# Empty slots left out of the product-row fetches, and fetch runs throttled to four, in a graph network kernel

## The chip, the cores and the metric

One NeuronCore of a Trainium2 chip runs the whole kernel. The metric is device time in microseconds for one execution, lower is better.

## The reference

The input is a graph of 1250 nodes (rows of 768 floats) and 20000 edges, each with a source, a destination and one of 34 relations. The network has two blocks, each added to its input:

```python
h = jnp.maximum(_layernorm(x), 0.0)
x = x + two_gatv2_layers_with_layer_norms(h)       # attention over the edges, 8 heads, then 1
h = jnp.maximum(_layernorm(x), 0.0)
# relational convolution and GCN
seg  = edge_type * n + dst
agg  = segment_sum(h[src], seg, 34 * n); cnt = segment_sum(ones, seg, 34 * n)
mean = agg / maximum(cnt, 1)
h1   = einsum('rni,rio->no', mean, W_rel) + h @ W_root + b
xw   = h1 @ W_gcn
out  = segment_sum(xw[src] * dinv[src] * dinv[dst], dst, n) + xw * dinv**2 + b2
x = x + out
```

## The kernel before, in words

The kernel is a row of stages; each ends in a barrier over all engines. In the trace of one execution they lie so: index (0 to 327 us), first attention (to about 890), settle_first (to 1120), attention_single (to 1559), settle_last (to about 1770), relation products (to about 2779), the sum of product rows (to 3153) and the GCN stage (to the end).

The index stage builds *group records*. Edges are sorted by destination; a group is 128 lanes of S=4 slots, each slot one edge of the lane's destination. 20000 edges need 44 groups, 11 turns of U=4, with 22528 slots, of which 2528 are empty; two more groups without any edge are only fetched. The first EARLY=48 records are completed in one run: GpSimd issues 48 indirect DMAs (lines 509 to 511) that fetch each lane's four edges, all counted on one semaphore, edges_in2; VectorE then zeroes what lies behind a lane's last edge (is_edge, L855 to L863), and SP stores the records (L426 to L427). Records beyond 48 go through a loop on GpSimd (L516 to L532). Before and after the run GpSimd scatters marks (mark, L216 to L223), each of which waits for the mark four before to have landed (MARKS=4). Meanwhile TensorE projects ten pairs of node tiles: a transpose (L171), ScalarE's copy of it (hT, L556), two half products of 36 matmuls (L178), and VectorE takes each from PSUM, adds the bias and sums heads (L673, L202); SP stores them.

settle_last is the like for the output of the second attention layer: tiles on TensorE, ScalarE (L1862 to L1880) and VectorE (L1954 to L1971), and on GpSimd 48 indirect DMAs (L1816 to L1818) that fetch, for the 48 groups' nodes, the row of reciprocal counts for all relations, then a loop for records beyond 48. VectorE turns these rows into the weight of each edge, later, by comparing the edge's relation, which it derives from the product-row key, with relation numbers.

The relation products write, for every (relation, node) pair, a product row of 768 floats to a table in DRAM, y_d; an edge's *key* is its row in it. In the sum stage (L2331 to L2476) the rows of each group's slots are fetched, weighted and summed by destination. Per group the engines do this:

- GpSimd (gather_rows, L967 to L991): runs ROWS_AHEAD=2 groups ahead with four indirect DMAs, one per slot, each a row for each of 128 lanes (rows_of, L889). It then scatters the sums of the group LAG=2 behind (sums_out, L942) with a bounds check, which drops lanes whose target lies outside the table, and copies this group's scatter targets out of the record (keep_target, L933), for which it waits until the scatter of the group four before has left its buffer.
- ScalarE: two scaled identity matrices (share, L2393), then two comparisons of sources with the node numbers (L2382, L2385).
- TensorE: eight matmuls that weight and sum the rows of two slots (L2413), and twelve that count sources (L2421).
- VectorE: two comparisons (L2445, L2448), the running sum with TensorE's part (L2460) and the rows of the other two slots (L2468), and the counts (L2473).
- SP loads the records (load_records, L945 to L965); a load waits for VectorE's counts of the group that held the buffer and for GpSimd's copied targets.

An empty slot has key 0, so row 0 of the table is fetched for it and gets weight 0. VectorE begins the stage with the bfloat16 identity (L2430), two memsets of sum buffers (L2432) and node numbers in half precision (L2434), and then opens the signals for which GpSimd's fetches wait.

Of the kernel before, what the change touches and what calls it, by code (L numbers as in the profile page):

```python
# [24 lines left out]
S = 4  # L25
# [12 lines left out]
MARKS = 4  # L38
EARLY = 48
CROWS = 2 * RELS  # L40
BIG = 1e30
# [35 lines left out]
def gnn_kernel(nc, io, out):  # L77
    ctx = ExitStack()
    with ctx:
# [163 lines left out]
        with stage() as st:  # L243
# [48 lines left out]
            rest_edge = sb("rest_edge", [P, S * 2], I32, st)  # L292
            early_in, edges_in2, masked, edges_out, rest_in, rest_step, rest_out = sems(
                st, "early_in", "edges_in2", "masked", "edges_out", "rest_in", "rest_step", "rest_out")
            p_index = pb("p_index", [P, 2, 512], F32, st)
# [61 lines left out]
            with nc.Block() as block:  # L357
                @block.sync
                def _(sp):
# [65 lines left out]
                    store(4, 0, P)  # L425
                    sp.wait_ge(masked, 2)  # L426
                    sp.dma_start(groups_d[:, 0:EARLY, :], early[:]).then_inc(edges_out, 16)  # L427
# [8 lines left out]
                def _(pool):  # L436
# [19 lines left out]
                    c.mark(pool.iota(relbase[:, 0:RELS], [[NP, RELS]], base=1, channel_multiplier=0, **iota))  # L456
                    c.mark(pool.memset(relbase[:, RELS:RELS + 1], BIG))
                    c.mark(pool.iota(arow[:], [[1, DA]], base=0, channel_multiplier=0, **iota))
# [49 lines left out]
                    pool.wait_ge(early_in, 16)  # L508
                    for g in range(EARLY):
                        pool.indirect_dma_start(early[:, g, 0:S * 2], None, table_rows, bass.IndirectOffsetOnAxis(  # L510
                            ap=early[:, g, R_ROW:R_ROW + 1], axis=0)).then_inc(edges_in2, 16)
                    for i in range(2, PROJ_COLS // 20):
                        mark_columns(i)
                    more = pool.value_load(ctl[0:1, C_REST:C_REST + 1], min_val=1, max_val=MAX_TURNS * U)
                    with pool.Fori(0, more) as k:
                        v = Steps(pool, rest_step, k * 2, posted)  # L516
# [12 lines left out]
                        v.link(pool.tensor_tensor(rest[:, 0:S * 2], rest[:, 0:S * 2], rest_edge[:], ALU.mult))  # L529
                        pool.dma_start(groups_d[:, ds(k + EARLY, 1), 0:S * 2].rearrange("p o c -> p (o c)"), rest[:, 0:S * 2])\  # L530
                            .then_inc(rest_out, 16)
# [117 lines left out]
                def _(dve):  # L649
# [210 lines left out]
                    dve.wait_ge(masked, 1)  # L860
                    dve.wait_ge(edges_in2, 16 * EARLY)
                    dve.tensor_tensor(edges, edges, is_edge[:], ALU.mult).then_inc(masked, 1)
                    evacuate(4, 1, LAST)  # L863

# [21 lines left out]

        def rows_of(pool, b, u, table, field, words):
            for j in range(S):
                pool.indirect_dma_start(b["row"][u][:, j, :].bitcast(words), None, table, bass.IndirectOffsetOnAxis(  # L889
                    ap=b["rec"][u][:, 2 * j + field:2 * j + field + 1], axis=0)).then_inc(b["row_in"][u], 16)  # L890

# [36 lines left out]
        def keep_target(pool, b, i, off):  # L928
# [37 lines left out]

        def gather_rows(pool, b, table, field, own, out_table, readers, done, words=F32):  # L967

            open_sums(pool, b)

            def fetch(i, off):
                u = off % U
                rec_wait(pool, b, i, off)
                for used in readers:
                    used.wait(pool, i, off - U)
                pool.sem_inc(b["posted"], 1)
                if own is not None:
                    own_of(pool, b, u, own)
                rows_of(pool, b, u, table, field, words)

# [3 lines left out]
            with pool.Fori(0, turns) as i:  # L984
                for u in range(U):
                    fetch(i, u + ROWS_AHEAD)
                    sums_out(pool, b, i, u - LAG, out_table, done)
                    keep_target(pool, b, i, u)
            for k in range(LAG, 0, -1):
# [692 lines left out]
        def settle_last(ahead):  # L1682
# [5 lines left out]
            with stage() as st:  # L1688
# [48 lines left out]
                    st, "den_in", "rden_ok", "cnt_in", "rcnt_ok", "rcnt_out", "rec_in")  # L1737
                crow_in, pool_step, rest_step, rest_out, rest_in = sems(
                    st, "crow_in", "pool_step", "rest_step", "rest_out", "rest_in")
                rel_const, present_in, summed, joined, seen_ok, seen_out, ntiles_ok, ends_ok, behind_ok, tile_ok = sems(  # L1740
# [6 lines left out]
                with nc.Block() as block:  # L1747
# [48 lines left out]
                    def _(pool):  # L1796
# [55 lines left out]
                        pool.sem_inc(posted, 1)  # L1852
                        pool.wait_ge(crow_in, 16 * EARLY)

# [477 lines left out]
        with stage() as st:  # L2332
# [12 lines left out]
            pR = pb("pR", [P, 2, 512], F32, st)  # L2345
            dve_step, node_ok, of_node_ok = sems(st, "dve_step", "node_ok", "of_node_ok")
            source_ok = Signal(st, "source_ok", 1, U, U)
# [10 lines left out]
            with nc.Block() as block:  # L2358
# [5 lines left out]
                def _(pool):  # L2364
                    pool.iota(node[:], [[1, NP]], base=1, channel_multiplier=0,
                              allow_small_or_imprecise_dtypes=True).then_inc(node_ok, 1)
                    gather_rows(pool, b, y_d, 1, None, ysum_d, (used, summed), (used, counted), I32)

                @block.scalar
                def _(act):  # L2370
# [17 lines left out]
                    with act.Fori(0, turns) as i:  # L2388
                        for u in range(U):
# [347 lines left out]
```

## Time and profile before

| | us |
|---|---|
| runs | 3357.39, 3352.17, 3353.75 |
| median | 3353.75 |
| profiled execution | 3372.56 |
| its span | 3371.1 |
| TensorE busy | 2760.3 |
| VectorE busy | 2187.0 |
| GpSimd busy | 1722.6 |
| ScalarE busy | 1617.7 |

The span is what the records cover of the profiled execution. "Busy" counts instructions at work; an engine's idle time is shown with what released it, and "issue" stands for time in which it waited for nothing that the profile shows. A wait for several semaphores is put down to the one that came last by the records. "PEclk", or the clock column of the windows, is the share of full speed granted to TensorE.

### The profile page before, as it was taken

The page shows a single profiled execution, that of the slowest core. Times are in us where ns is not written, and L with a number is a line of the kernel's source. Part 1 is how long each engine was busy: PE and PEld are TensorE (multiplying, and loading weights), DVE is VectorE, ACT ScalarE, POOL GpSimd, SP SyncE. Part 2 cuts the span into 40 slices and gives each one's busy share as a digit, 9 for nine tenths or more (in the row PEclk, how much of TensorE's full clock was granted, in tenths as well). Part 3 has the DMA queues.
Part 4 walks back from the last instruction along what each step waited for, and adds up shares of the span by engine and source line. Part 5 has one row for each costly group of instructions (what it writes and reads, how often), then busy time and mean ns, then how long its engine had stood idle before and what let it go on. Part 6 is the DMA issues. An engine that isn't in the chain of part 4 may idle for free. (4 is left out here: it accounts for less than half of the span.)

```text
span 3371.1 us, 53614 instructions
## 1 busy us (share of the span) xinstructions
PE 2760.3 (82%) x11962; PEld 2042.9 (61%) x11985; DVE 2187.0 (65%) x3989; ACT 1617.7 (48%) x5047; POOL 1722.6 (51%) x2089
## 2 busy tenths in 40 slices
PE   5637789888689799995377999999999976676599
PEld 3314445454345455552247999999999973333499
DVE  6503789989666689884365666566566646767554
ACT  0000799999622133331344655656665556767100
POOL 3660556556477588883503444444444436767200
PEclk9859899999889899996698999999999998888799
DMA  4212546555442577775228777777777756667412
GB/s 141 84 18 91 175 151 182 168 170 174 155 120 81 168 230 227 233 231 186 66 91 267 231 245 240 235 237 243 232 244 237 239 129 213 211 218 221 151 62 85
DMA packets 212101, 596.86 MB, mean 177 GB/s; under 512 B 75813, under 2 KB 78905, under 8 KB 211871
## 3 DMA queue, kind: packets, MB, share of 16 engines
q0 software_dynamic: 96256, 380.68, 36.2%
q1 hardware_dynamic: 93487, 163.45, 15.6%
q10 hardware_dynamic: 22304, 52.11, 4.9%
q8 instruction: 22, 0.36, 0.0%
q14 instruction: 32, 0.26, 0.0%
HBM read 491.85 MB, written 161.57 MB: 194 GB/s over the span
## 5 line engine op out<-in xcount | busy, mean ns | idle before, releaser
L2263 PE MATMUL pO<-wh,gT 128*128 128x384 f32 x3264 | 867.9, 340 | 20.8 <-ACT gT L2214 8.3
L2263 PEld LDWEIGHTS pO<-wh,gT 128*128 128x128 f32 x3264 | 593.4, 188 | 26.6 <-issue 13.8
L2263 PE MATMUL pO<-wl,gT 128*128 128x384 f32 x1632 | 546.6, 335 | 0.0
L889 POOL DMA_INDIRECT row<-fs_d,rec x368 | 436.6, 1186 | 113.7 <-issue 112.5
L2279 DVE TENSOR_SCALAR cut<-pT 128x768 int32<-128x768 int32 x137 | 131.0, 956 | 373.1 <-ACT gT L2214 197.2
L1090 ACT ACTIVATE sj<-sj 128x96 f32<-128x96 f32 x1080 | 287.6, 268 | 62.1 <-DVE sj L1202 57.2
L178 PE MATMUL pO<-wt,hT 128*128 128x384 f32 (+1 forms) x720 | 254.6, 512 | 65.8 <-issue 31.4
L2263 PEld LDWEIGHTS pO<-wl,gT 128*128 128x128 f32 x1632 | 307.9, 189 | 0.0
L2214 ACT ACTIVATE gT<-cut 128x256 fp32r<-128x256 f32 x822 | 291.9, 410 | 28.1 <-DVE cut L2282 4.3
L2413 PE MATMUL pR<-row,share 128*128 128x384 f32 x352 | 148.7, 574 | 121.0 <-DMA row<-y_d,rec 39.5
L178 PEld LDWEIGHTS pO<-wt,hT 128*128 128x128 f32 (+1 forms) x720 | 141.9, 199 | 172.9 <-issue 89.8
L889 POOL DMA_INDIRECT row<-y_d,rec x184 | 195.4, 1062 | 92.5 <-issue 47.1
L1128 PE MATMUL pS<-row,ident 128*128 128x384 f32 x368 | 162.7, 525 | 96.1 <-DVE sj L1202 67.0
L222 POOL DMA_INDIRECT marked_d<-marks,recc x160 | 205.6, 1285 | 64.7 <-issue 49.9
L1360 PE MATMUL pA<-row,share 128*128 128x384 f32 x704 | 234.4, 486 | 0.1
L1149 PE MATMUL pA<-row,ident 128*128 128x384 f32 x704 | 234.2, 486 | 0.0
L178 PE MATMUL pO<-settle_wt,hT 128*128 128x384 f32 x480 | 172.4, 519 | 70.2 <-ACT hT L1880 49.8
L2139 POOL DMA_INDIRECT g<-hr_d,gindex x138 | 159.2, 1153 | 126.7 <-POOL keys L2136 74.5
L1090 ACT ACTIVATION_READ_ACCUMULATOR sj<-sj 128x1 f32 x1080 | 202.1, 187 | 8.0 <-issue 8.0
L2203 ACT ACTIVATE sign<-startrow,after 128x1279 bf16<-128x1279 f16 (+1 forms) x139 | 188.4, 1355 | 27.5 <-DMA startrow<-seen_d 26.4
L2292 DVE TENSOR_TENSOR wl<-raw,wh 128x768 fp32r<-128x768 f32 x204 | 195.5, 959 | 7.0
L2133 POOL TENSOR_SCALAR sourcef<-total 128x1 f32<-128x1 f32 x138 | 30.6, 221 | 322.6 <-ACT sign L2203 320.2
(388 smaller groups left out, 5626.6 us busy)
## 6 DMA issues: line engine op xcount, KB each, us to landing
raw<-in_L_gnn_W_rel_dram SPq DMA_DIRECT2D x204, 384.0 KB
startrow<-seen_d ACTq DMA_DIRECT2D x141, 320.0 KB
fs_d<-of SPq DMA_DIRECT2D x18, 388.0 KB
fd_d<-of SPq DMA_DIRECT2D x18, 388.0 KB
row<-fs_d,rec POOLq DMA_INDIRECT x368
ha<-first_d SPq DMA_DIRECT2D x10, 384.0 KB
ha<-second_d SPq DMA_DIRECT2D x10, 384.0 KB
kept_d<-y SPq DMA_DIRECT2D x10, 384.0 KB
```

The costliest lines, as they stand in the source:

```text
L178: last = pe.matmul(dst[0:rows, q, 0:HALF], rows_t[:, c * P:c * P + rows], w[:, c, lo:up], start=c == 0, stop=c == KC - 1)
L222: pool.indirect_dma_start(marked_d[k], bass.IndirectOffsetOnAxis(ap=keys, axis=0), marks[0:EP], None)\
L889: pool.indirect_dma_start(b["row"][u][:, j, :].bitcast(words), None, table, bass.IndirectOffsetOnAxis(ap=b["rec"][u][:, 2 * j + field:2 * ...
L1090: last = act.activation(of_head, of_head, ACT.Copy, accum_out=dots[off % U][:, j, h:h + 1])
L1128: pe.matmul(pS[j][:, q, 0:HALF], ident[:], row[off % U][:, S // 2 + j, lo:up], start=True, stop=False)
L1149: last = pe.matmul(pA[:, q, 0:HALF], ident[:], row[u][:, j, lo:up], start=j == 0, stop=j == S - 1)
L1360: last = pe.matmul(pA[u % 2][:, q, 0:HALF], share[u % 2][:, 1 + j, :], row[u][:, j, lo:up], start=j == 0, stop=False)
L2139: pool.indirect_dma_start(g[:, b, :], None, hr_d, bass.IndirectOffsetOnAxis(ap=gindex[b][:], axis=0))\
L2203: act.activation(sign[:, 0:COUNT[b]], seen_row[b][:, 0:COUNT[b]], ACT.Sign, bias=half, scale=-1.0, accum_out=total[b][:]).then_inc(total_o ...
L2214: act.activation(gT[:, c].bitcast(F32R), cut[:, :, c * P:(c + 1) * P], ACT.Copy).then_inc(gT_ok.sem, 1)
L2263: last = pe.matmul(pO[:, q, 0:HALF], gT[:, c, half, :].bitcast(F32R), w[:, c, lo:up].bitcast(F32R), start=c == 0 and k == 0, stop=c == KC ...
L2292: dve.tensor_tensor(wl[b][:, c, :].bitcast(F32R), raw[b * KC + c], wh[b][:, c, :], ALU.subtract).then_inc(w_ok.sem, 1)
```

## The change

1. *Throttled runs.* The semaphores edges_in2 and crow_in become OPEN=4 each. In both runs of 48 fetches, fetch g counts on semaphore g % 4, and from the fifth on GpSimd waits, before it issues one, until the fetch four before has landed.
2. *Empty slots get a key outside the table.* NO_ROW is RELS * NP + 1. VectorE sets the keys of empty slots to it with two more operations in the index stage, GpSimd with two more in the loop for records beyond 48. The last relation base becomes NO_ROW in place of 1e30.
3. *Fetches with a bounds check.* In the sum stage lanes whose key is out of bounds are left out of the fetch. Their buffers keep what was there, so VectorE clears the four row buffers first.
4. *Scatter targets copied by ScalarE*, behind its comparisons, in place of GpSimd. Only the sum stage does so; the attention stages keep GpSimd's copy.

```diff
+OPEN = 4
+NO_ROW = RELS * NP + 1
...
-                    sp.wait_ge(masked, 2)
+                    sp.wait_ge(masked, 4)
...
-                    c.mark(pool.memset(relbase[:, RELS:RELS + 1], BIG))
+                    c.mark(pool.memset(relbase[:, RELS:RELS + 1], float(NO_ROW)))
...
                     for g in range(EARLY):
+                        if g >= OPEN:
+                            pool.wait_ge(edges_in2[g % OPEN], 16 * (g // OPEN))
                         pool.indirect_dma_start(early[:, g, 0:S * 2], None, table_rows, bass.IndirectOffsetOnAxis(
-                            ap=early[:, g, R_ROW:R_ROW + 1], axis=0)).then_inc(edges_in2, 16)
+                            ap=early[:, g, R_ROW:R_ROW + 1], axis=0)).then_inc(edges_in2[g % OPEN], 16)
...
+                        v.link(pool.tensor_scalar(rest_edge[:], rest_edge[:], -float(NO_ROW), float(NO_ROW), ALU.mult, ALU.add))
+                        keys = rest[:, 0:S * 2].rearrange("p (s c) -> p s c", c=2)[:, :, 1]
+                        v.link(pool.tensor_tensor(keys, keys, rest_edge[:].rearrange("p (s c) -> p s c", c=2)[:, :, 1], ALU.add))
...
                     dve.tensor_tensor(edges, edges, is_edge[:], ALU.mult).then_inc(masked, 1)
+                    dve.wait_ge(masked, 2)
+                    keys = edges.rearrange("p g (s c) -> p g s c", c=2)[:, :, :, 1]
+                    of_key = is_edge[:].rearrange("p g (s c) -> p g s c", c=2)[:, :, :, 1]
+                    dve.scalar_tensor_tensor(out=keys, in0=of_key, scalar=-float(NO_ROW), in1=keys, op0=ALU.mult, op1=ALU.add)\
+                       .then_inc(masked, 1)
+                    dve.wait_ge(masked, 3)
+                    dve.tensor_scalar(keys, keys, float(NO_ROW), None, ALU.add).then_inc(masked, 1)
...
+        def target_by_act(act, b, i, off):
+            u = off % U
+            rec_wait(act, b, i, off)
+            sum_free(act, b, i, off)
+            act.activation(b["to"][u][:], word(b, u, R_OUT), ACT.Copy).then_inc(b["to_ok"][u], 1)
...
                         for g in range(EARLY):
+                            if g >= OPEN:
+                                pool.wait_ge(crow_in[g % OPEN], 16 * (g // OPEN))
                             pool.indirect_dma_start(crow[:, g, :], None, rcnt_d, bass.IndirectOffsetOnAxis(
-                                ap=crec[:, g, R_NODE:R_NODE + 1], axis=0)).then_inc(crow_in, 16)
+                                ap=crec[:, g, R_NODE:R_NODE + 1], axis=0)).then_inc(crow_in[g % OPEN], 16)
...
-                    gather_rows(pool, b, y_d, 1, None, ysum_d, (used, summed), (used, counted), I32)
+                    pool.wait_ge(rows_clear, U)
+                    gather_rows(pool, b, y_d, 1, None, ysum_d, (used, summed), (used, counted), I32, targets=False,
+                                bounds_check=RELS * NP, oob_is_err=False)
...
                             for k in range(S - BY_DVE):
                                 compare(i, u, k)
+                            target_by_act(act, b, i, u)
...
+                    for u in range(U):
+                        dve.memset(row[u][:], 0.0).then_inc(rows_clear, 1)
                     pre = Steps(dve, dve_step)
```

## Rows read from the trace of the kernel before

**Rows 1.** Page, part 1: busy time, share and instructions of each engine, whole span.

```profile
PE 2760.3 (82%) x11962; PEld 2042.9 (61%) x11985; DVE 2187.0 (65%) x3989; ACT 1617.7 (48%) x5047; POOL 1722.6 (51%) x2089
```

**Rows 2.** Windows: engines' busy us, TensorE clock, DMA share, GB/s, six stretches.

```profile
212.00:245.00 33.00, 6.23 (x11) 2.24 (x10) 0.00 (x0) 0.00 (x0) 24.48 (x22) 0.50 0.08 1
...
262.00:306.00 44.00, 41.20 (x140) 24.40 (x139) 17.18 (x113) 4.74 (x7) 0.00 (x0) 1.00 0.23 79
...
940.00:1060.00 120.00, 113.65 (x365) 67.22 (x364) 79.64 (x130) 29.13 (x34) 93.70 (x76) 0.98 0.31 87
1592.00:1617.00 25.00, 23.27 (x52) 10.27 (x50) 7.92 (x17) 8.31 (x10) 19.13 (x19) 0.63 0.30 75
1617.00:1655.00 38.00, 0.00 (x0) 0.00 (x0) 0.00 (x0) 0.00 (x0) 28.16 (x31) 0.55 0.13 14
...
2780.00:3145.00 365.00, 242.61 (x858) 125.89 (x880) 253.15 (x315) 255.18 (x264) 258.61 (x277) 0.86 0.70 216
```

**Rows 3.** Waits, 151 to 262: engine, line, releaser: us, times, longest.

```profile
DVE of L673 <- issue: 65.1, 1, 65.1
```

**Rows 4.** Timeline, 192 to 251: start, us, engine, line, operation, idle before.

```profile
192.74 1.13 PE L178 MATMUL pO<-wt,hT 128*128 128x384 f32 x3
...
240.35 1.18 POOL L222 DMA_INDIRECT marked_d<-marks,recc  x1 [0.30 <-issue]
...
249.97 0.50 PEld L178 LDWEIGHTS pO<-wt,hT 128*128 128x128 f32 x2 [9.65 <-issue]
```

**Rows 5.** Timeline, 1615 to 1663.

```profile
1615.43 0.82 PE L171 MATMUL pT<-ident,ht 128*128 128x128 f32 x6
...
1661.37 0.81 ACT L1880 ACTIVATE hT<-pT 128x768 f32<-128x768 f32 x1 [48.07 <-DMA by_dst_d<-by_dst_d]
...
1662.23 1.01 PE L178 MATMUL pO<-settle_wt,hT 128*128 128x384 f32 x1 [45.99 <-ACT hT L1880]
```

**Rows 6.** Lines, 940 to 1000 and 1592 to 1655: busy us, mean ns, idle.

```profile
L222 POOL DMA_INDIRECT marked_d<-marks,recc x35 | 45.7, 1306 | 14.2 <-issue 10.4 <-POOL recc L1570 2.0 <-DMA marked_d<-marks,recc 1.9
...
L1817 POOL DMA_INDIRECT crow<-rcnt_d,crec x48 | 46.7, 972 | 32.0 <-DMA rcnt_d<-rcnt 17.7 <-issue 14.3
```

**Rows 7.** First crow fetch in the timeline; DMA share in slices of 0.1 us, 1592 to 1596.

```profile
1592.38 1.02 POOL L1817 DMA_INDIRECT crow<-rcnt_d,crec  x1 [17.67 <-DMA rcnt_d<-rcnt]
...
DMA  0000000000000000200059510000000007830000
```

**Rows 8.** Timeline, 306 to 328, end of the index stage.

```profile
306.61 0.56 DVE L862 TENSOR_TENSOR early<-early,is_edge 128x384 int32<-128x384 int32 x1
312.59 0.96 DVE L673 TENSOR_TENSOR of<-pO,bias 98x768 f32<-98x768 f32 x1 [5.43 <-PE pO L178]
...
327.16 0.22 POOL L925 IOTA to<- 128x1 int32 x2 [70.90 <-POOLq L152]
```

**Rows 9.** Timeline, 2779 to 2785, start of the sum stage.

```profile
2781.44 1.23 DVE L2432 MEMSET sum<- 128x1408 f32 x1 [0.24 <-issue]
...
2784.33 1.00 POOL L889 DMA_INDIRECT row<-y_d,rec  x1 [3.76 <-DVEq L234]
```

**Rows 10.** Lines, 2778 to 3153, the sum stage.

```profile
L889 POOL DMA_INDIRECT row<-y_d,rec x184 | 195.4, 1062 | 92.5 <-issue 47.1 <-DMA rec<-groups_d 34.7 <-DVEq L234 3.8
...
L942 POOL DMA_INDIRECT ysum_d<-sum,to x46 | 49.5, 1076 | 13.9 <-issue 12.6 <-DVE sum L2468 0.6 <-DMA rec<-groups_d 0.3
...
L933 POOL COPY to<-rec 128x1 int32<-128x1 int32 x44 | 14.3, 325 | 0.0
```

**Rows 11.** Timeline, 3046 to 3065, one stall in the sum stage.

```profile
3052.71 1.02 POOL L942 DMA_INDIRECT ysum_d<-sum,to  x1 [0.30 <-issue]
...
3059.15 1.02 POOL L942 DMA_INDIRECT ysum_d<-sum,to  x1 [0.30 <-issue]
...
3063.15 1.55 DVE L2473 SCALAR_TENSOR_TENSOR sum<-sum,rec,pC 128x1280 int16<-128x1280 int16 x1 [11.89 <-DMA marked<-marked_d]
```

**Rows 12.** DMA queues, 2780 to 3145: packets, MB, share of 16 engines.

```profile
q0 software_dynamic: 20859, 78.52, 68.4%
```

More of the change, by code:

```diff
@@ L292, in gnn_kernel @@
             rest_edge = sb("rest_edge", [P, S * 2], I32, st)
-            early_in, edges_in2, masked, edges_out, rest_in, rest_step, rest_out = sems(
-                st, "early_in", "edges_in2", "masked", "edges_out", "rest_in", "rest_step", "rest_out")
+            edges_in2 = sems(st, *[f"edges_in2_{k}" for k in range(OPEN)])
+            early_in, masked, edges_out, rest_in, rest_step, rest_out = sems(
+                st, "early_in", "masked", "edges_out", "rest_in", "rest_step", "rest_out")
             p_index = pb("p_index", [P, 2, 512], F32, st)
@@ L515, in _ @@
                     with pool.Fori(0, more) as k:
-                        v = Steps(pool, rest_step, k * 2, posted)
+                        v = Steps(pool, rest_step, k * 4, posted)
                         pool.wait_ge(rest_out, k * 16)
@@ L860, in _ @@
                     dve.wait_ge(masked, 1)
-                    dve.wait_ge(edges_in2, 16 * EARLY)
+                    for landed in edges_in2:
+                        dve.wait_ge(landed, 16 * (EARLY // OPEN))
                     dve.tensor_tensor(edges, edges, is_edge[:], ALU.mult).then_inc(masked, 1)
+                    dve.wait_ge(masked, 2)
[5 more added lines that the diff above has]
+                    dve.tensor_scalar(keys, keys, float(NO_ROW), None, ALU.add).then_inc(masked, 1)
                     evacuate(4, 1, LAST)
@@ L885, in word, with rows_of @@
             return b["rec"][u][:, c:c + 1].bitcast(dt)
-        def rows_of(pool, b, u, table, field, words):
+        def rows_of(pool, b, u, table, field, words, **last):
             for j in range(S):
                 pool.indirect_dma_start(b["row"][u][:, j, :].bitcast(words), None, table, bass.IndirectOffsetOnAxis(
-                    ap=b["rec"][u][:, 2 * j + field:2 * j + field + 1], axis=0)).then_inc(b["row_in"][u], 16)
+                    ap=b["rec"][u][:, 2 * j + field:2 * j + field + 1], axis=0), **last).then_inc(b["row_in"][u], 16)
         def own_of(pool, b, u, table):
@@ L965, in load_records, with gather_rows @@
                 sp.sem_inc(b["sp_posted"], 1)
-        def gather_rows(pool, b, table, field, own, out_table, readers, done, words=F32):
+        def gather_rows(pool, b, table, field, own, out_table, readers, done, words=F32, targets=True, **last):
             open_sums(pool, b)
@@ L978, in fetch @@
                     own_of(pool, b, u, own)
-                rows_of(pool, b, u, table, field, words)
+                rows_of(pool, b, u, table, field, words, **last)
             for off in range(ROWS_AHEAD):
@@ L987, in gather_rows @@
                     sums_out(pool, b, i, u - LAG, out_table, done)
-                    keep_target(pool, b, i, u)
+                    if targets:
+                        keep_target(pool, b, i, u)
             for k in range(LAG, 0, -1):
@@ L1737, in settle_last @@
                     st, "den_in", "rden_ok", "cnt_in", "rcnt_ok", "rcnt_out", "rec_in")
-                crow_in, pool_step, rest_step, rest_out, rest_in = sems(
-                    st, "crow_in", "pool_step", "rest_step", "rest_out", "rest_in")
+                crow_in = sems(st, *[f"crow_in{k}" for k in range(OPEN)])
+                pool_step, rest_step, rest_out, rest_in = sems(
+                    st, "pool_step", "rest_step", "rest_out", "rest_in")
                 rel_const, present_in, summed, joined, seen_ok, seen_out, ntiles_ok, ends_ok, behind_ok, tile_ok = sems(
@@ L1852, in _ @@
                         pool.sem_inc(posted, 1)
-                        pool.wait_ge(crow_in, 16 * EARLY)
+                        for landed in crow_in:
+                            pool.wait_ge(landed, 16 * (EARLY // OPEN))
                     @block.scalar
@@ L2345, in gnn_kernel @@
             pR = pb("pR", [P, 2, 512], F32, st)
-            dve_step, node_ok, of_node_ok = sems(st, "dve_step", "node_ok", "of_node_ok")
+            dve_step, node_ok, of_node_ok, rows_clear = sems(st, "dve_step", "node_ok", "of_node_ok", "rows_clear")
             source_ok = Signal(st, "source_ok", 1, U, U)
```

## The prediction

> **What bounds the kernel now.** I read the page's parts 1 and 2 first, then the windows by stage, then the waits of the stages that the diff touches, and last the timeline around their longest waits. The kernel is a row of stages with a barrier between them, so a saving counts only in the stage where it falls. Over the whole span TensorE has most to do, 82%, and GpSimd 51% [rows 1]. Nearly half of the span, the two attention layers and the relation products, is outside the diff and I hold it fixed. The profiled execution took 3372.6 us, 18.8 more than the median of 3353.75; I make the sum against 3372.6 and subtract 18.8 at the end.
>
> Three stretches matter. The first is the index stage (0 to 327), where TensorE projects tiles while GpSimd sorts edges. Here GpSimd issues the 48 early fetches of line 510 back to back and then twenty marks of line 222. VectorE does nothing from 180 to 245: one wait of 65.1 us [rows 3], put down to "issue", so that no producer was late by the records. From 212 to 245 TensorE gets through 11 matmuls in 33 us at the half clock, 0.50, with the DMA engines 8% busy [rows 2]. Before and after, it is the path: 41.2 of 44 us busy from 262 to 306 at clock 1.00 [rows 2]. The second is settle_last, where GpSimd issues the 48 fetches of line 1817, each 0.97 us with 14.3/47 = 0.30 us between two [rows 6]. From 1617 to 1655 TensorE, its weight loads, VectorE and ScalarE are busy for 0.00 us, with DMA at 13% [rows 2]. ScalarE's copy of hT waits 48.07 us for transposes that were over long before, and TensorE's product waits 45.99 us for that copy [rows 5]. Both stalls end within a few microseconds of the end of GpSimd's run.
>
> The third is the sum stage (2779 to 3153). No engine is full there: TensorE 243, VectorE 253, ScalarE 255 and GpSimd 259 us of 365, DMA 70% [rows 2]. Its 44 groups take 8.1 us each ((3140.7 - 2784.3)/44, from the first row fetch to the last turn), while GpSimd when nothing holds it takes 3059.15 - 3052.71 = 6.44 us [rows 11]. The rest is again waits with nothing late in the records: VectorE 11.89 us ahead of line 2473, ended by a DMA that has nothing to do with this stage [rows 11].
>
> **The change part by part.**
> *Throttle in the index stage.* What does a run of fetches do to the others when each fetch waits for the fourth before it? The trace has such a run: the marks of line 222 wait in exactly this way. From 940 to 1060, in settle_first, some 70 of them were issued at 1306 ns each with gaps of 0.3 [rows 6], and beside them TensorE was busy for 113.65 of 120 us at clock 0.98 [rows 2]. The two runs without the wait both stopped everybody. That speaks for the wait as the cure. If the stall goes, TensorE, whose matmuls still came at 0.32 to 0.38 us each at 193 (three in 1.13 us), needs for the rest of its half product and the transposes, 17 matmuls that the timeline shows crawling from 196 to 242, about 11 x 0.32 + 6 x 0.14 = 4.4 us, ScalarE 0.81 for the copy, and is back at the next product at about 199.5 in place of 249.97 [rows 4]: **-50 us**. Bounds: 0 (nothing cured) and -65 (VectorE's whole wait). The next to be late would be GpSimd. It ended 70.9 us before 327.16 [rows 8], so it has 20 us left. The added waits cost it nothing that decides: a mark has the same gap of 0.30 as a fetch [rows 4, 6].
>
> *Mask.* VectorE gets two operations on half the elements of the mask's (0.56 us each for 128x384 [rows 8]), together 0.6 to 1.2 us. Behind the mask it waits 5.43 us for TensorE [rows 8]; that hides them: 0. In GpSimd's rest loop two operations of 0.2 to 0.3 us: 0 to 1, in its slack: 0. The store of the records by SP waits for them, and is followed by 15 us of the stage: 0.
>
> *Throttle in settle_last.* If cured, TensorE goes on right behind its transposes, which end at 1616.25, plus 0.81 for the copy and 0.1: 1617.2 in place of 1662.23 [rows 5]: -45, less about 1 for the clock: **-44 us**. Bounds 0 and -48. GpSimd's fetches and the rest loop then run beside tiles, and it has no work in the rest of the stage: hidden.
>
> *Clearing the row buffers.* Four memsets of 128x3072 ahead of everything VectorE does at the start of the sum stage. One of 128x1408 takes 1.23 us [rows 9]; the smaller ones of the trace give the same 0.83 to 0.91 ns an element, so 3072 take 2.6 us, four 10.5. GpSimd's first fetch waits for VectorE's opening of the stage (3.76 us idle, released by VectorE [rows 9]), which now comes behind the memsets: nothing hides them. **+10.5** (bounds +8 and +12.5).
>
> *Bounds check on 184 fetches.* The scatter of line 942 carries a check already and takes 1.02 where a fetch takes 0.94 to 1.00 [rows 9, 11]; so 0 to 0.08 us each, 0 to +15 in all, if GpSimd is the bound throughout. It is so for part of the stage: **+6**.
>
> *Target copy off GpSimd.* It loses 0.325 us per group [rows 10] and 0.15 of gap and gets 0.30 of gap back: 0.18 x 44 = 8, for part of the stage: **-5** (0 to -8). ScalarE gets about 0.2 us per group; it is busy 255.18 of 365 [rows 2], and its new wait, for the buffer's store four groups ago, is one VectorE makes anyway. Behind it in ScalarE's queue stands the next group's share, for which TensorE waits: 0, up to +9 (0.2 x 44) if ScalarE is late.
>
> *Fewer bytes.* Of the 22528 slots of 44 groups 20000 hold edges, and the two groups fetched ahead hold none; 3552 of 23552 rows (15%) are not moved, 10.9 of 78.52 MB [rows 12]. TensorE or VectorE seldom wait for rows as such, DMA stands at 68.4% [rows 12], and GpSimd issues as many instructions as before: **-8** (0 to -30), and -2 for the tail, where the last two groups' fetches are still moving rows behind the last sum.
>
> Sum stage: 10.5 + 6 - 5 - 8 - 2 = +1.5. Total -50 - 44 + 1.5 = -92.5: 3372.6 - 92.5 = 3280.1, less 18.8: **3261 us**.
>
> **The rivals.**
> 1. *The wait never blocks.* A fetch starts at 1592.38 and its packets run from 1594.0 to 1594.4 [rows 7], 2 us later; four fetches take 4 x 1.25 = 5.0 us to issue. So the fourth before has always landed, the same fetches go out at the same times, and whatever in a dense run starves the others stays. For it: the marks from 212 to 245 wait in just this manner, at 1.18 us with gaps of 0.30 [rows 4], and the stall went on through them. Against it: the marks at 940 to 1060, and that without the wait GpSimd's sequencer may run further ahead of its DMAs, which the wait forbids even when it is short. Time: 3353.75 + 1.5 = 3355, within 3335 to 3375 by the sum stage's bounds.
> The Trainium skill, "DMA: Bandwidth & Descriptors", section "Anatomy of one DMA — SWDGE (gpsimd) path", gives such a DMA a fixed cost of about 2.0 us, for the most part completion; by it too the wait would be inert. [...]
> 2. *One of the two is cured, or each by half.* The two stalls differ: the index stage's has marks behind the fetches that keep it alive from 212 to 245, so only its first half may go. -44 or -50 alone, or -47 by halves: 3308.
> 3. *Slower.* The wait is inert, GpSimd is the bound of the sum stage by its dense issue, and the stage gets +10.5 from the memsets, +15 from the checks, +5 from ScalarE's new copy standing ahead of the share, and -5 for the copy gone: +25, 3379. It decides as soon as the checks cost over 0.05 us each and the missing bytes give nothing. For it: 6.44 us of GpSimd per group in dense stretches is the nearest thing to a bound [rows 11]. Against: the average is 8.1.
>
> **How the numbers follow.** Forecast 0.42, rival 1 0.37, rival 2 0.13, rival 3 0.08. The likeliest one's own range is 3235 to 3290. The range reaches from 3240 through rivals 2 and 1 to 3370, leaving out little of the forecast's low side and rival 3 and the top of rival 1. I call 0.2% (6.7 us) the least that a measurement here tells from none. Rival 1 is centred at no change with its sum uncertain by 15: faster 0.3, within 0.3, slower 0.4 of it. Faster: 0.42 + 0.13 + 0.11 = 0.66, which I lower to 0.61, as a mechanism of which I see only the coincidence may fail in ways I have not listed; the same 0.12; slower 0.27.
>
> **What would show it.** Right: VectorE's wait at line 673 near 180 and TensorE's near 1616 are gone; windows over both fetch runs show TensorE above 70% busy and a clock near 1; the index stage ends near 277 and settle_last is 44 us shorter; the sum stage is about as long as before, with its first row fetch 14 to 15 us behind the barrier, up from 5. Wrong: line 510's fetches still run at 1.25 us beside idle engines (rival 1); the index stage alone keeps its stall (rival 2); mean of line 889's fetches above 1.1 us and a sum stage of 390 us or more (rival 3). If the sum stage shortens by more than 20 us, the missing bytes were worth more than I gave them.

## The result, and the profile after

The changed kernel takes 3362.34 us (median of 20 runs, 3346.24 to 3382.20) against 3352.91 of the kernel before (median of 20, 3339.40 to 3365.16). The ratio is 1.0037, with a 95% interval of 1.0021 to 1.0052: 7 to 17 us slower. I had forecast 3261, with 0.61 on faster. Two of the experiments below had one execution each far above their others (7325.80 us in change_with_two, 3897.76 in sum_pause_every_second), which their ratios leave out.

The profiled execution of the changed kernel took 3349.36 us, 13 below its own median, and the profiled one of before 19.7 above its median of 20. The two spans (3347.8 and 3371.1) therefore say the opposite of the comparison; only stages can be compared. First the windows, whose columns are the stretch, its length, busy us of PE, PEld, DVE, ACT and POOL, TensorE's clock, DMA share and GB/s. They answer to [rows 2]:

```profile
212.00:245.00 33.00, 1.85 (x5) 0.91 (x5) 2.48 (x17) 0.00 (x0) 24.25 (x23) 0.50 0.10 13
...
262.00:306.00 44.00, 41.21 (x140) 24.23 (x139) 17.55 (x101) 4.75 (x7) 0.00 (x0) 1.00 0.25 88
...
940.00:1060.00 120.00, 112.59 (x373) 67.04 (x372) 78.15 (x126) 30.78 (x34) 93.72 (x77) 1.00 0.33 93
1592.00:1617.00 25.00, 22.61 (x69) 12.89 (x68) 15.76 (x32) 15.52 (x19) 19.52 (x19) 0.82 0.39 108
1617.00:1655.00 38.00, 11.10 (x36) 6.46 (x33) 9.67 (x21) 7.67 (x10) 27.76 (x31) 0.69 0.25 65
```

The index stage's stall is as it was: TensorE does 5 matmuls in 33 us at clock 0.50. In settle_last TensorE is busy for 11.10 of the 38 us from 1617, where it did nothing before; the experiments show how far this varies by itself. VectorE's wait at its first bias addition, now line 681, is the one of [rows 3] again:

```profile
DVE of L681 <- remote: 73.5, 2, 59.0
```

and the throttled fetches, in the timeline, have the spacing they had without a throttle, 1.25 us with gaps of 0.30:

```profile
155.18 0.95 POOL L515 DMA_INDIRECT early<-by_dst_d,early  x1 [0.30 <-issue]
156.43 0.94 POOL L515 DMA_INDIRECT early<-by_dst_d,early  x1 [0.30 <-issue]
```

The sum stage starts, in the timeline, so (for [rows 9]):

```profile
2743.41 2.62 DVE L2461 MEMSET row<- 128x3072 f32 x1 [24.78 <-PEq L154]
...
2753.03 2.62 DVE L2461 MEMSET row<- 128x3072 f32 x1 [0.59 <-issue]
...
2760.43 1.07 POOL L905 DMA_INDIRECT row<-y_d,rec  x1 [4.50 <-issue]
```

The stage begins at 2742.4, so the first row fetch comes 18.0 us behind it; before, 5.2 (2779.2 to 2784.33). The clears take 4 x (2.62 + 0.59) = 12.8 us. Behind the first fetch the stage runs on for 369.6 us (to 3130.0), against 369.2 before (2784.3 to 3153.5). One profile could not show this, as this length varies: over the nine profiles that leave the fetches alone (before, clears_only, and the throttles and breaks in the two fetch runs below) it is 361 to 374, with a mean of 369.2; over the four with checks, copy and missing bytes it is 364 to 374, with a mean of 369.4. So the three come to nothing in sum, as far as this can be seen. Their rows, groups by line, for [rows 10]:

```profile
L905 POOL DMA_INDIRECT row<-y_d,rec x184 | 197.7, 1074 | 106.0 <-issue 52.8 <-DMA rec<-groups_d 30.2 <-DVE sum L2501 17.1
...
L965 POOL DMA_INDIRECT ysum_d<-sum,to x46 | 49.4, 1075 | 14.9 <-issue 13.1 <-DVE sum L2506 1.5 <-DVE sum L2501 0.3
...
L956 ACT ACTIVATE to<-rec 128x1 int32<-128x1 int32 x44 | 8.3, 188 | 1.5 <-DMA ysum_d<-sum,to 1.5
```

The queue moved 10.5 MB less than in [rows 12], from 2743 to 3122:

```profile
q0 software_dynamic: 21029, 68.05, 56.9%
```

Its packets did not become fewer, 21029 against 20859. A lane that is left out still counts with 4 bytes: behind the first fetch, the trace of before has row packets of 6144 bytes (two lanes) alone, and the changed kernel's has 1740 of 8 bytes and 72 of 3076 in their place, which makes exactly the 3552 lanes.

### The profile page after: what moved, and what is told of

The parts are those of the page before. It is cut to its first block and busy times, and to the rows that moved or that the text cites. A ratio compares the mean times of both kernels' runs of the same rounds, so it can differ in the third digit from the quotient of the medians.

```text
span 3347.8 us, 53835 instructions
## 1 busy us (share of the span) xinstructions
PE 2769.2 (83%) x11984; PEld 2043.5 (61%) x11985; DVE 2198.2 (66%) x3995; ACT 1624.1 (49%) x5091; POOL 1720.3 (51%) x2047
## 5 line engine op out<-in xcount | busy, mean ns | idle before, releaser
L2444 PE MATMUL pR<-row,share 128*128 128x384 f32 x352 | 158.1, 604 | 127.6 <-DVE sum L2493 52.9
L224 POOL DMA_INDIRECT marked_d<-marks,recc x160 | 206.5, 1291 | 64.8 <-issue 53.0
L2444 PEld LDWEIGHTS pR<-row,share 128*128 128x128 f32 x352 | 78.9, 236 | 185.4 <-issue 135.7
```

The lines of the kernel that those rows point to most:

```text
L224: pool.indirect_dma_start(marked_d[k], bass.IndirectOffsetOnAxis(ap=keys, axis=0), marks[0:EP], None)\
L2444: last = pe.matmul(pR[:, q, 0:HALF], share[u % 2][:, k, :], row[u][:, BY_DVE + k, lo:up], start=k == 0, stop=k == S - BY_DVE - 1)
```

## Experiments

Each kernel is timed against the kernel before on the same chip; a ratio carries its 95% interval. The last three columns come from each profile: TensorE's busy us in the window 180 to 250, the end of the index stage, and settle_last's length, both by the first instructions of the stages.

| kernel | ratio | TensorE, 180 to 250 | index ends | settle_last |
|---|---|---|---|---|
| before | 1 | 24.6 | 327 | 208 |
| changed (OPEN=4) | 1.0037 (1.0021 to 1.0052) | 13.1 | 325 | 188 |
| throttle_only (OPEN=4) | 0.9996 (0.9979 to 1.0013) | 20.6 | 325 | 208 |
| three_in_flight | 0.9985 (0.9967 to 1.0004) | 23.0 | 326 | 201 |
| two_in_flight | 0.9768 (0.9739 to 0.9796) | 27.3 | 300 | 162 |
| one_in_flight | 1.0014 (0.9996 to 1.0033) | 63.1 | 334 | 196 |
| bursts_of_12 | 0.9762 (0.9729 to 0.9794) | 41.0 | 299 | 164 |
| bursts_of_4 | 0.9750 (0.9722 to 0.9778) | 64.8 | 291 | 164 |
| breaks_by_work | 0.9745 (0.9717 to 0.9774) | 64.9 | 285 | 165 |
| change_with_two | 0.9800 (0.9775 to 0.9825) | 50.2 | 276 | 163 |
| bursts_of_8_clears_in_time | 0.9735 (0.9713 to 0.9756) | 64.9 | 273 | 168 |

**The throttle.**

```diff
 (throttle_only: the kernel before with part 1 of the change, OPEN = 4)
-OPEN = 4
+OPEN = 1      # one_in_flight; 2 and 3: two_in_flight, three_in_flight
```

> The kernel before with the two throttled runs alone: four semaphores each, and from the fifth fetch on a wait for the one four before. Theory A (the wait never blocks, since a fetch lands about 2 us after issue and four take 5 us): ratio to before 1.000 within 0.003; in the profile the 48 fetches still come every 1.25 us, VectorE still waits 50 us or more at the line of its first bias addition near 180, and TensorE or ScalarE 20 us or more in settle_last. Theory B (my forecast: the throttle lets the others run): 80 to 95 us less, ratio 0.973 to 0.976, and neither wait is there. Theory C (it cures settle_last alone, as the profile of the changed kernel hinted, whose settle_last was 20 us shorter): ratio 0.988 to 0.994.

> As throttle_only, but with each fetch waiting for the one before it (one semaphore, OPEN=1), so that the wait must block: a fetch every 2.5 to 3.2 us, the index run 120 to 155 us long in place of 60, settle_last's likewise. If the density of GpSimd's issue starves the others (the pauses of 1.5 to 2 us free them), VectorE and TensorE work on beside both runs; the index stage is then bound by GpSimd, 151 + 140 + marks 32 + rest 13 = about 336 us against 327, settle_last ends 35 to 45 us sooner: total -25 to -40, ratio 0.988 to 0.993. If the stall has nothing to do with how dense the run is, it lasts as long as the run, and the total rises by 100 us or more, ratio above 1.03.

> The kernel before with both fetch runs on OPEN=2 semaphores: each fetch waits for the one two before. A fetch lands about 2.5 us after issue and two take 2.5 us to issue, so this wait blocks hardly or not. If the pauses are what frees the others (one_in_flight paused 1.6 us after each fetch and had no stall), the fetches stay near 1.25 to 1.4 us apart, the stall of 50 us or more in the index stage is still there, ratio 0.99 to 1.00. If it is the number in flight (2 against 4), the stall is gone: index stage 270 to 285 us, ratio 0.975 to 0.98.

> The kernel before with OPEN=3 in both runs. Three fetches take 3.75 us to issue and one lands about 2.5 us after issue, so the wait never blocks, while at OPEN=2 it blocked now and then (gaps of 0.4 to 2.5 us). If only a wait that really blocks helps, ratio 0.997 to 1.002 as with four. If a smaller number ahead helps without blocking, ratio below 0.99.

With four or three nothing happens to the time. Theory A holds: the wait never blocks. From the first to the last fetch of the index run there are 1.25 us per fetch in all three kernels (before, four, three). Theory C falls: settle_last was 208 us long with the throttle alone, and between 188 and 209 in the profiles of all kernels whose stall was not cured, so the 20 us in the profile of the changed kernel were chance. With one in flight the stall is gone, as the window from 180 to 250 shows, then the waits to 300:

```profile
180.00:250.00 70.00, 63.11 (x206) 35.95 (x204) 20.72 (x121) 5.98 (x9) 23.60 (x25) 0.99 0.24 74
```

```profile
POOL early L514 <- DMA early<-by_dst_d,early: 86.7, 47, 5.2
DVE early L867 <- DMA early<-by_dst_d,early: 49.4, 1, 49.4
```

TensorE is busy 63 of 70 us and through with its tiles by 250. But GpSimd now idles 86.7 us behind landings, its run ends near 280, and VectorE waits for it: the stage ends at 334. Of the 25 to 40 us that I expected from this kernel settle_last gave some 12 by its profile, which is within the spread of the uncured ones, and the index stage took 7; the total did not move measurably. With two, where I had expected the stall to stay if pauses are what counts, the time falls by 2.3%. The timeline shows why: this wait does block, for 0.1 to 2.2 us at a time.

```profile
158.75 0.94 POOL L514 DMA_INDIRECT early<-by_dst_d,early  x1 [1.09 <-DMA early<-by_dst_d,early]
...
169.08 0.94 POOL L514 DMA_INDIRECT early<-by_dst_d,early  x1 [2.48 <-DMA early<-by_dst_d,early]
```

In the index stage, which ends at 300, it helps by half only; VectorE still has one wait of 33.9 us:

```profile
DVE of L677 <- remote: 45.8, 2, 33.9
```

**Breaks.**

```diff
 (bursts_of_12, bursts_of_4, against throttle_only: BURST 12 or 4, all landed before the next burst; in both runs)
-                        if g >= OPEN:
-                            pool.wait_ge(edges_in2[g % OPEN], 16 * (g // OPEN))
+                        if g and g % BURST == 0:
+                            for landed in edges_in2:
+                                pool.wait_ge(landed, 16 * (g // OPEN))
 (breaks_by_work: on the kernel before, no throttle, in both runs)
+                        if g and g % 4 == 0:
+                            pool.wait_ge(filled, g // 4 - 1)      # its own work four fetches ago
+                            pool.iota(spare[:].rearrange("p a b -> p (a b)"), [[1, 12 * NSPARE]], ...)   # 1920 numbers
```

> The kernel before with both runs cut into four bursts of 12 fetches (15 us each) and a wait for all of them to have landed between two bursts (a pause of about 1.6 us); inside a burst nothing waits. If a pause every 15 us is enough to let the other engines take up their work, as in the runs of ten marks with 1.0 us between, which stalled nobody in settle_first, the index stage ends near 275 to 285 us and settle_last is 30 to 40 us shorter: ratio 0.973 to 0.980. If a pause must come after every fetch, the stall stays nearly whole, ratio 0.995 to 1.000.

> As bursts_of_12 with bursts of 4: 5 us of issue, 1.6 us of pause, the run of 48 about 77 us. If the pause frees the others at all between one and twelve fetches, this kernel shows it: no stall, index stage 280 to 290 us, settle_last 30 to 40 us shorter, ratio 0.975 to 0.982. If only fetches one at a time do, a stall of 30 us or more stays in the index stage and the ratio is above 0.99.

> The kernel before with no throttle at all, but with about 1.8 us of GpSimd's own work (numbers written to a spare tile) behind every four fetches of both runs, without a wait for any landing. If a break in the issue of fetches is what lets the others run, it cures as bursts_of_4 did: ratio 0.975 to 0.985, with no wait of VectorE over 20 us in the index stage. If GpSimd must stand idle in a wait, the stall stays and its run is 20 us longer beside it: ratio 0.997 to 1.005, VectorE's wait 50 us or more.

The windows from 180 to 250, of bursts_of_12, bursts_of_4 and breaks_by_work in turn:

```profile
180.00:250.00 70.00, 40.99 (x111) 23.21 (x110) 13.34 (x80) 3.77 (x6) 49.80 (x50) 0.76 0.20 47
```

```profile
180.00:250.00 70.00, 64.77 (x210) 37.01 (x210) 26.96 (x165) 6.50 (x10) 39.35 (x41) 1.00 0.31 89
```

```profile
180.00:250.00 70.00, 64.85 (x211) 37.01 (x210) 26.87 (x160) 6.79 (x10) 57.22 (x53) 1.00 0.31 89
```

In the third GpSimd is busier than in any other kernel, 57 of 70 us, and never waits for a landing between fetches; its eleven breaks are work, as the groups by line from 148 to 235 show:

```profile
L517 POOL DMA_INDIRECT early<-by_dst_d,early x47 | 45.3, 963 | 14.7 <-issue 12.5 <-DMA by_dst_d<-by_dst_d 2.3
L515 POOL IOTA spare<- 128x1920 f32 x11 | 19.3, 1751 | 7.0 <-issue 7.0
```

Still TensorE is busy 65 of 70 us at full clock. So an idle GpSimd is not needed: a break in the issue of indirect DMAs cures the stall. Nor is a small number in flight enough, since with OPEN=3 there are never more than three and the stall stays. Twelve in a row (15 us) are too many for the index stage, which ends at 299 where I expected 275 to 285; eight (below) and four are not. The timeline of bursts_of_12 shows VectorE's causeless waits ending about when GpSimd's drains do, and the next one growing within the next burst:

```profile
185.03 0.95 POOL L516 DMA_INDIRECT early<-by_dst_d,early  x1 [2.17 <-issue]
185.47 0.96 DVE L679 TENSOR_TENSOR of<-pO,bias 128x768 f32<-128x768 f32 x1 [12.38 <-remote]
...
201.85 0.95 POOL L516 DMA_INDIRECT early<-by_dst_d,early  x1 [2.12 <-DMA early<-by_dst_d,early]
202.56 0.96 DVE L679 TENSOR_TENSOR of<-pO,bias 128x768 f32<-128x768 f32 x1 [14.55 <-remote]
```

A third wait, of 20.1 us to 232.43, stands beside the marks that follow the fetches.

One rival is left. Every break also slows the mean pace of issue, and no run here separates the two. From the first to the last fetch of the index run there are, per fetch, 1.25 us before; 1.37 in bursts_of_12 and 1.40 in two_in_flight, where part of the stall is left; 1.46 in change_with_two and in bursts_of_8_clears_in_time; 1.79 in breaks_by_work and 1.80 in bursts_of_4. That breaks count and not the pace alone is supported by the ends of the waits above; by two_in_flight, which is slower than bursts_of_12 and yet stalls more (TensorE busy 27.3 us against 41.0); and by the two kernels with 1.46 us: with the irregular pauses of change_with_two VectorE still has a wait of 13.6 us, with a drain after every eight fetches none above 5.2. A run with an even 1.6 us between fetches, and no breaks, was not made.

**The clears.**

```diff
 (clears_only: on the kernel before)
+                    pool.wait_ge(rows_clear, U)
                     gather_rows(pool, b, y_d, 1, None, ysum_d, (used, summed), (used, counted), I32)
 ...
                     for s in (source_ok, equal_dve, added):
                         s.open(dve)
+                    for u in range(U):
+                        dve.memset(row[u][:], 0.0).then_inc(rows_clear, 1)
 (clears_just_in_time: on the changed kernel)
             for off in range(ROWS_AHEAD):
+                if clear is not None:
+                    pool.wait_ge(clear, off + 1)
                 fetch(0, off)
+            if clear is not None:
+                pool.wait_ge(clear, U)
 ...
-                    for u in range(U):
-                        dve.memset(row[u][:], 0.0).then_inc(rows_clear, 1)
+                    dve.memset(row[0][:], 0.0).then_inc(rows_clear, 1)
+                    used.open(dve)
                     pre = Steps(dve, dve_step)
 ...
                     dve.sem_inc(of_node_ok, 1)
-                    used.open(dve)
                     counted.open(dve)
+                    for u in range(1, U):
+                        dve.memset(row[u][:], 0.0).then_inc(rows_clear, 1)
```

> The kernel before with nothing but VectorE's four clears of the row buffers ahead of the sum stage's start, and GpSimd's wait for them. If they explain the change's loss, the first row fetch comes 18 us behind the stage's start in place of 5, the sum stage is 12 to 14 us longer (386 to 388 us), ratio 1.003 to 1.005, the same as the whole change. If the loss came from the bounds checks, the scatter targets on ScalarE or the index stage, this kernel is within 5 us of the one before at 1.000 to 1.0015, with a sum stage at most 5 us longer.

> The changed kernel with one clear ahead of the first fetch and the other three behind VectorE's start-up work, each fetch waiting only for its own buffer's clear, and the signal that lets the fetches start opened at once. If the clears' place is all that costs, the first row fetch comes 3 to 5 us behind the stage's start and the sum stage takes 370 to 375 us, ratio 0.999 to 1.001 and 10 to 15 us under the changed kernel. If the checks and the copy cost as well (rival 3), it stays above 1.002.

clears_only has a ratio of 1.0058 (1.0041 to 1.0075), 14 to 25 us, somewhat above what the 12.8 us of clears explain; the whole change has no more than that. Its first fetch comes 17.9 us behind the stage's start, as expected; the profiled stage is 379 us long and not 386 to 388, because it has only 361 behind that fetch, the low end of the spread given above. clears_just_in_time is at 1.0005 (0.9991 to 1.0020), some 11 us under the changed kernel (1.0037, 1.0021 to 1.0052) by the two ratios. Its timeline from 2766.1, where its sum stage begins:

```profile
2767.07 2.62 DVE L2463 MEMSET row<- 128x3072 f32 x1 [24.19 <-PEq L154]
...
2770.65 1.07 POOL L905 DMA_INDIRECT row<-y_d,rec  x1 [3.17 <-DVE row L2463]
...
2774.31 2.62 DVE L2474 MEMSET row<- 128x3072 f32 x1 [0.92 <-DVE of_node L2470]
```

The first fetch is 4.6 us behind the stage's start, and the other clears run beside fetches.

**The checks.**

```diff
 (checks_only: on the kernel before; empty slots keep key 0, which is in bounds)
-                    gather_rows(pool, b, y_d, 1, None, ysum_d, (used, summed), (used, counted), I32)
+                    gather_rows(pool, b, y_d, 1, None, ysum_d, (used, summed), (used, counted), I32,
+                                bounds_check=RELS * NP, oob_is_err=False)
```

> The kernel before with the bounds check on the sum stage's 184 row fetches, and nothing else: the keys of empty slots stay 0, in bounds, so that no lane is left out and no clear is needed. If a check costs 0.08 us and GpSimd is the bound: the fetches' shortest time 1.02 in place of 0.94 us, sum stage 10 to 15 us longer, ratio 1.003 to 1.0045. If the price is nothing or hidden: sum stage 370 to 378 us, ratio 0.999 to 1.001; then what the missing bytes and the copy on ScalarE bring is nothing either, since the changed kernel behind its first fetch took as long as the one before.

The line's own view gives shortest, median and longest:

```profile
  L889 POOL DMA_INDIRECT row<-y_d,rec x184: 997/1005/1772, 2765.5 to 3134.9; - x184
```

A check costs GpSimd 0.055 us (0.997 against 0.942 for the shortest fetch before), 10 us for 184, but the total is 0.9987 (0.9963 to 1.0012), so between 12 us less and 4 us more. The profile's sum stage was 387 us long, against 366 to 379 in the kernels that leave the stage alone; the total doesn't bear that out. What the checks cost the kernel stays open within these 12 and 4 us.

**Breaks in the sum stage.** There are five kernels, all on the kernel before.

```diff
 (sum_pause_each_group; sum_pause_every_second only for u in (1, 3))
                     fetch(i, u + ROWS_AHEAD)
+                    rows_wait(pool, b, i, u + ROWS_AHEAD)
 (sum_pause_by_scatter; v is the scatter's buffer)
                     sums_out(pool, b, i, u - LAG, out_table, done)
+                        pool.wait_ge(b["sum_out"][v], i * 16 + 16 * ((u - LAG) // U + 1 + (v >= U - LAG)))
 (sum_work_each_group; sum_work_every_second: 1920 numbers, u in (1, 3))
                     fetch(i, u + ROWS_AHEAD)
+                        pool.iota(work[0][:], [[1, 1280]], base=0, channel_multiplier=0, ...)
```

> The kernel before with GpSimd waiting, behind each group's four row fetches in the sum stage, until they have landed (about 2 us), before it scatters the sums of an earlier group. GpSimd's shortest time per group rises from 6.4 to about 8.5 us. If the stalls of VectorE, TensorE and ScalarE in that stage are of the same kind as those beside the two fetch runs, they go (slow instructions of SP, 0.7 us, too), and the stage is bound by GpSimd: 44 x 8.5 = 374 us, as before, ratio 0.997 to 1.003. If they are of another kind, both add: 44 x 10 = 440 us, ratio above 1.015.

> As sum_pause_each_group, but only behind every second group: a pause every 13 us, GpSimd's shortest time 7.4 us per group. If a pause every 12 to 15 us keeps the others running, as in bursts_of_12, the stage takes 330 to 350 us in place of 374, ratio 0.988 to 0.993. If the stalls are of another kind: 374 + 44 us or so, ratio above 1.005.

> The kernel before with GpSimd waiting in the sum stage, behind each group's scatter of sums, until that scatter has landed. In sum_pause_each_group the wait was for 393 KB of rows and took 4.4 us; the scatter is a tenth of that group's traffic behind the same queue. If it waits for the whole queue in front of it all the same, the pause is again 4 us or more and the stage 480 us or more, ratio above 1.03. If it is short (1 to 2 us), GpSimd's time per group is 7.5 to 8.5 us and the stage 330 to 375 us, ratio 0.987 to 1.000.

> The kernel before with 1.2 us of GpSimd's own work behind each group's four row fetches in the sum stage, and no wait for any landing. GpSimd's shortest time per group rises from 6.4 to 7.9 us. If the stage's stalls come from unbroken issue, as beside the two fetch runs, they go, and the stage takes what GpSimd then needs: 44 x 7.9 + 15 = 363 us against 374, ratio 0.994 to 1.000. If they come from the queue full of rows, which breaks_by_work had not, they stay, and the stage is 40 to 60 us longer, ratio 1.010 to 1.018.

> As sum_work_each_group, with 1.8 us of work behind every second group: GpSimd's shortest time 7.5 us per group, a break every 13 us. If unbroken issue is the cause and one break in 13 us is enough, the stage takes 44 x 7.5 + 15 = 345 us, ratio 0.990 to 0.995. If the queue full of rows is the cause: 20 to 45 us longer, ratio 1.005 to 1.014.

The pauses that wait for a landing fail: 1.0429 (1.0404 to 1.0454), 1.0163 (1.0135 to 1.0191) and 1.0321 (1.0292 to 1.0351), with stages of 510, 426 and 491 us. GpSimd waits 4.5 us for a group's rows (193.8 us in 43 waits; four times the 393 KB that I had written) and 3.1 for a scatter (137.2 in 44), against 6.4 us of work per group, and becomes the bound. That the scatter lands late because it stands behind the rows in the same queue is my reading; no run shows it. GpSimd's wait for the scatter, in the waits of sum_pause_by_scatter:

```profile
POOL to L933 <- DMA ysum_d<-sum,to: 132.3, 43, 4.8
```

Breaks by work leave the time as it was, 1.0012 (0.9989 to 1.0034) and 1.0007 (0.9987 to 1.0026), but change what it is made of. The waits of sum_work_each_group from 2780 to 3120:

```profile
ACT far L2390 <- DVE source L2453: 68.1, 34, 4.1
DVE sum L2468 <- PE pR L2421: 61.6, 22, 5.2
PE pR L2421 <- issue: 51.9, 22, 3.3
```

VectorE has no long wait without a cause any more (the longest is 3.6 us, before 11.89 [rows 11]); it waits for TensorE, in pieces of at most 5.2 us. TensorE's own causeless waits became shorter, at most 3.3 us against 8.1, but not less in sum, 51.9 against 35.4. From its first fetch on GpSimd waits for nothing longer than 1.5 us and sets the pace: its scatters come every 8.0 us, where dense stretches before had 6.44, and the stage takes 374.6 us, against 374.3. I had expected 363. So the long stalls there give way to breaks like those beside the fetch runs, which makes the same kind of stall likely but does not show it, and a break of 1.2 us per group costs what it brings.

**Both findings together.**

```diff
 (change_with_two: on the changed kernel)
-OPEN = 4
+OPEN = 2
 (bursts_of_8_clears_in_time: the changed kernel with BURST = 8 and the clears as above)
```

> The changed kernel with one number altered: OPEN is 2 in place of 4. If the throttle was right in kind and only its size too loose, this takes what two_in_flight took off the kernel before and adds what the changed kernel's clears cost: 0.977 + 0.004, ratio 0.979 to 0.983, index stage about 300 us, settle_last about 162. If something else in the change keeps the stall, ratio above 0.99.

> The changed kernel with bursts of 8 fetches between drains in place of the throttle, and the clears just in time. If both findings add up: the 0.975 of the bursts times the 1.0005 of clears_just_in_time, ratio 0.973 to 0.978, index stage 280 to 290 us, settle_last about 163, sum stage 366 to 378. Above 0.98 one of the two does not carry over.

Both ratios came out as expected, 0.9800 (0.9775 to 0.9825) and 0.9735 (0.9713 to 0.9756), though the index stages ended sooner than I thought, at 276 and 273 in place of about 300 and 280 to 290. The second is the best kernel of the study, at 3258.87 us. Its window from 180 to 250:

```profile
180.00:250.00 70.00, 64.88 (x206) 36.76 (x204) 25.62 (x147) 5.97 (x9) 49.12 (x49) 0.98 0.32 89
```

## Why the prediction was wrong

- *What the stalls are worth*: right. I had -50 and -44. breaks_by_work took 42 off the index stage and 43 off settle_last in its profile, and 2.55% (2.26 to 2.83), 86 us, off the whole; the best kernel's index stage is 55 us shorter.
- *"That speaks for the wait as the cure"*: this step failed, for both stages. Rival 1, the wait that never blocks, is what happened, and its working (2 us to the packets, 5.0 us to issue four) was sound. The 2 us are to the end of the packets, which start 1.6 us after the fetch [rows 7]; in one_in_flight the next fetch starts 2.5 us after the last, so that of these 2.5 us at most some 0.9 come after the packets have begun to move, and most of the time to land is not completion here. I read the marks of settle_first [rows 6] as a throttled run without a stall and gave the credit to the throttle. They have two other things in common with what works. After ten of them GpSimd copies the next columns and leaves a gap of 1.0 us (the row's "POOL recc L1570 2.0", two such), a break every 16 us or so; and they come every 1.6 us, the fetches every 1.25. Which of the two keeps settle_first free no run here shows. The evidence against my reading stood in the same trace: the marks from 212 to 245, throttled likewise, did not end the stall, nor did the gaps of 1.0 us before and between their tens. So marks do not start a stall (those from 33 to 66, every 1.49 us, stand beside a TensorE that is busy 28.4 of 33 us) and do not end one at once.
- *The likeliest case by a hair*: with the pattern of issue unchanged to 0.01 us, a forecast of 94 us needed a mechanism in which a wait that does not block alters something. I named one (the sequencer running ahead) and had no row for it. Its chance should have been far under 0.42.
- *Clears*: +10.5 forecast, 12.8 measured; the missing part is the gap of 0.59 us behind each memset, which the memset of [rows 9] shows smaller, 0.24.
- *Checks, copy, bytes, tail*: +6 - 5 - 8 - 2 = -9 forecast, 0 measured, in the changed kernel's profile (369.6 against 369.2) and in the means of four and nine profiles (369.4 against 369.2). 13% fewer bytes bring nothing that can be seen, as hardly anyone waited for rows: in the sum stages TensorE waited 39.5 us for rows before and 52.2 after, of which 33.5 and 46.0 are the first wait of the stage. The check costs GpSimd 0.055 us, within my 0 to 0.08, and does not show in the total; ScalarE's copy takes 0.188 us and nobody waits for it.
- *Mask*: hidden, as forecast; the index stage did not grow (325 against 327).
- The time of rival 1, 3355, is within 8 us of 3362. The clears were too kind by 2.3 us and the sum stage's other terms by 9, which is more than enough for the rest.

## What to carry to other kernels

Ask of every added wait whether it ever blocks, by issue spacing times depth against the time to land; where it did not, with four or three in flight, it changed nothing here, whatever the company in which such a wait had been seen. A setup step at a stage's head goes on the path in full if the first transfer waits for all of it; let each transfer wait for its own part. When two stretches of a trace differ in stalling, list everything in which they differ (here the wait, the gaps and the pace) before crediting one, and try the cheapest: here a few lines were worth 2.5%.

## What the runs showed of the hardware

A run of indirect DMAs issued by GpSimd without a break, one per 1.25 us, after 15 to 25 us brings the other engines nearly to a halt, with the DMA engines 8% busy [rows 2]: matmuls at one per 2.8 us, semaphore waits that end long after their producer [rows 5], and SP's DMA issues of 0.70 us. The one of h_d below took 0.34 us in bursts_of_4, where nothing stalls (before, timeline of SP from 166 and of TensorE from 226):

```profile
166.54 0.33 SPq L369 DMA_DIRECT2D fd_d<-of  x1
171.44 0.70 SPq L362 DMA_DIRECT2D xt<-in_x_dram  x1
175.64 0.71 SPq L366 DMA_DIRECT2D h_d<-ht  x1
...
226.83 0.37 PE L171 MATMUL pT<-ident,ht 128*128 128x128 f32 x1 [1.99 <-issue]
229.63 0.37 PE L171 MATMUL pT<-ident,ht 128*128 128x128 f32 x1 [2.43 <-issue]
```

A break of 1.8 us after four, or a drain of 2.2 us after eight, prevents it; whether a slower even pace would do as well was not tried. By what path GpSimd's issue holds up the others, no run here shows.
